# A hand-written schedule: weight preparation placed behind the second block's transposed queries

## The reference

```python
x = x + layernorm(attn(layernorm(x)))      # attn: h = h + global(rmsnorm(h)); h = h + local(rmsnorm(h))
x = x + layernorm(ffn(layernorm(x)))
# global: 16 query heads, 4 key heads of 8, latent keys and values, causal mask, rope and norm of q and k
# local:  the same head shape, each token sees the 32 tokens up to itself
# ffn:    h = layernorm(x) * gamma + beta
#         shared expert silu(h @ q(sw1).T) @ q(sw2).T, plus top_prob * expert[argmax router](h), 8 experts
#         q(W): scale = mean|W| per row;  clip(round(W / scale), -1, 1) * scale
```

## Time and profile before

| | |
|---|---|
| median of 3 runs | 808.54 us (807.95 to 810.76) |
| span of the profiled execution | 806.6 us |
| median less span | 1.9 us |
| PE matmul busy | 579.3 us, 72% of the span |
| DVE busy | 468.5 us, 58% |
| ACT busy | 363.7 us, 45% |
| POOL busy | 348.6 us, 43% |

### The profile page before, as it was taken

The page is one execution under the profiler, slowest core; times in us unless marked ns, Lnnn a source line. Parts: engine busy times, 40 slices in busy tenths (PEclk is TensorE's granted clock), DMA queues, the critical chain, the costliest instruction groups (busy, mean ns, idle before and its releaser), DMA issues.

```text
span 806.6 us, 15564 instructions
## 1 busy us (share of the span) xinstructions
PE 579.3 (72%) x5544; PEld 282.4 (35%) x5621; DVE 468.5 (58%) x1130; ACT 363.7 (45%) x482; POOL 348.6 (43%) x752
## 2 busy tenths in 40 slices
PE   1217727838688877989898898978898898665353
PEld 1103313416243434444434343433343332422241
DVE  5473867665678566676566745683266221656256
ACT  0013404423446436746675567647764787103000
POOL 3504786486335573557326432653004530045200
PEclk9956867978899989999999999999999999765566
DMA  7000000000000000000000000000000000000000
GB/s 207 1 0 1 1 2 1 1 1 2 1 8 1 2 1 8 2 2 5 4 2 1 5 5 2 2 4 5 2 2 1 8 2 1 1 0 8 1 0 7
DMA packets 8809, 6.20 MB, mean 8 GB/s; under 512 B 1816, under 2 KB 8096, under 8 KB 8736
## 3 DMA queue, kind: packets, MB, share of 16 engines
q10 hardware_dynamic: 3424, 2.69, 1.2%
q1 hardware_dynamic: 5312, 2.52, 1.2%
HBM read 4.16 MB, written 1.05 MB: 6 GB/s over the span
## 4 chain that ended last, share of the span: by engine, by line
PE 26%; POOL 25%; DVE 23%; issue 18%; another core or an unknown queue 5%; ACT 1%; DVEq 0%; SPq 0%; DMA 0%; POOLq 0%; ACTq 0%
PE osum_g L893 8%; POOL prob L677 8%; PE scores L869 7%; DVE qT L1213 3%; PE misc L990 3%; DVE early L1321 3%; PE misc L1001 2%; POOL qe_g L652 2%; DVE acc L1363 2%; POOL prob L670 1%; POOL qe_l L652 1%; POOL ke_g L657 1%; DVE early L1360 1%; POOL rs_g L600 1%
## 5 line engine op out<-in xcount | busy, mean ns | idle before, releaser
L739 ACT ACTIVATE prob<-scores 128x1024 f32<-128x1024 f32 (+3 forms) x352 | 314.8, 925 | 191.0 <-PE scores L869 146.1
L869 PE MATMUL scores<-qT,kT 128*128 128x512 bf16 (+3 forms) x693 | 179.1, 353 | 43.9 <-DVEq L1217 19.6
L893 PE MATMUL osum_g<-prob,V 128*32 128x256 f32 (+1 forms) x2304 | 171.9, 385 | 10.1 <-ACT prob L739 4.6
L677 POOL TENSOR_TENSOR prob<-prob,band 128x768 f32<-128x768 f32 (+1 forms) x64 | 98.8, 1574 | 80.1 <-ACT prob L739 80.1
L869 PEld LDWEIGHTS scores<-qT,kT 128*128 128x128 bf16 x760 | 50.9, 100 | 146.9 <-issue 118.0
L893 PEld LDWEIGHTS osum_g<-prob,V 128*32 128x32 f32 x2304 | 51.1, 109 | 97.4 <-issue 81.0
L670 POOL TENSOR_SCALAR_AFFINE_SELECT prob<-prob 128x512 f32<-128x512 f32 x64 | 41.2, 664 | 88.1 <-ACT prob L739 87.9
L1001 PE MATMUL misc<-t2T,h1p 128*128 128x512 bf16 x182 | 53.2, 451 | 24.8 <-DVE h1p L1353 19.9
L1213 DVE COPY qT<-misc 64x1024 bf16<-64x1024 bf16 x64 | 44.1, 689 | 13.6 <-PE misc L855 8.2
L990 PE MATMUL misc<-early,t1T 128*128 128x256 bf16 x384 | 47.5, 285 | 2.8 <-DVEq L1325 2.6
L893 PE MATMUL misc<-prob,V 128*32 128x128 f32 (+2 forms) x736 | 31.5, 288 | 18.5 <-POOL prob L677 18.0
(11 more groups left out here) (212 smaller groups left out, 838.5 us busy)
## 6 DMA issues: line engine op xcount, KB each, us to landing
X<-in_L_attn_hidden_dram SPq DMA_DIRECT2D x8, 128.0 KB, 5.0
early<-in_L_ffn_expert_w_dram ACTq DMA_DIRECT2D x1, 1024.0 KB, 7.3
out_dram<-X SPq DMA_DIRECT2D x16, 64.0 KB, 1.5
rope<-in_rope_dram SPq DMA_DIRECT2D x1, 256.0 KB, 3.5
early<-in_L_ffn_shared_w_dram ACTq DMA_DIRECT2D x2, 128.0 KB, 9.2
band<-in_band_dram ACTq DMA_DIRECT2D x1, 96.0 KB, 3.0
wraw_l<-in_L_attn_l_wq_dram ACTq DMA_DIRECT2D x1, 64.0 KB, 2.5
ident<-in_ident_dram SPq DMA_DIRECT2D x1, 64.0 KB, 2.3
```

The source lines that it names most:

```text
L677: pool.tensor_tensor(d, d, m.unsqueeze(1).broadcast_to([P, 4, n]), ALU.mult).then_inc(mask_done, 1)
L739: act.activation(prob[:, n % NP, :, lo:hi], src, ACT.Exp, scale=float(HD) ** -0.5).then_inc(exp_done, 1)
L869: ins = pe.matmul(o[:, :, c:c + w], kT[a][:, g, P * (t % kept[a]):P * (t % kept[a]) + P], qT[a][:, b % Q_KEPT[a], 2 * g + m, :, q:q + w], ...
L893: ins = pe.matmul(o[32 * m:32 * m + 32, q:q + w], V[a][:, t % kept[a], g, :], prob[:, n % NP, m, c:c + w], start=(first and k == 0), stop= ...
```

## The change

Two steps of the feed chain, `prep` and `ternary` 0, are not allowed until the second half of block 1's query transposition (`qT`, G, 1, 1) is in the list. The rule that the first local block needs `prep` moves from its projection to its norm. `prep` has a name of one element, for which `allowed` did not ask `reads_done`; now it does. No operation is added, removed or altered; only the list can differ.

```diff
     def reads_done(s):
 
+        if s in (("prep",), ("ternary", 0)):
+            return ("qT", G, 1, 1) in plan
         kind, a, *at = s
...
-        if kind == "proj" and a == L and ("prep",) not in plan:
+        if kind == "norm" and a == L and ("prep",) not in plan:
             return False
...
     def allowed(s):
-        return (s[0] != "qk" or room(2)) and (s[0] != "pv" or s[1:] in ended) and banks(s) and (len(s) == 1 or reads_done(s))
+        return (s[0] != "qk" or room(2)) and (s[0] != "pv" or s[1:] in ended) and banks(s) and (len(s) == 1 and s != ("prep",) or reads_done(s))
```

## The result

The changed kernel takes 828.72 us, median of 4 runs (824.93 to 830.83), against 808.93 us of the kernel before on the same chips: ratio 1.0258, 95% interval 1.0218 to 1.0298. It was forecast 8 us faster and is 20 us slower, outside the range. The profile after is of the fastest of the four (824.93 us), so the two traces differ by 16.6 us of span and not by 20.

A forecast was written before the change was run, and what follows sets the result against it. Bound by the PE stream from 200 to 700 us, by DVE and POOL block preparation from 78.8 to 112.7. Span 806.6 - 11.8 + 0 + 3.4 + 0 + 0 = 798.2, with 1.9 around it 800.1 us; range 789 to 811.

The forecast's parts named there:

- Step 1: Start of the kernel: preparation leaves the path of block 0's key copy, first scores at 44.7 us; -11.8 us.
- Step 2: Block 0's attention and block 1's copies: all moves forward in one piece; 0 taken, bounds 0 to -7 us.
- rival C: Better than a shift: block 1's copies move by 19 us instead of 12; 793.1 us, chance 0.14.
- Step 3: Preparation put back behind block 1's query copies, DVE idle time taking up part; +3.4 us, bounds 0 to +11.8.
- Step 4: First ternary step's eight compares at the new place, with POOL at work: no longer; 0 taken, other end 9.9 us.
- Step 5: Feed-forward weights slide by at least 26 us, first local block by at most 11.8; both covered, cost 0.
- Step 6: From 200 us to the end: the early gain is let through in full.
- The reservation: In step 6: the greedy planner makes all later choices anew, and in-order waits may vanish or appear; no size given.
- The sign named for this step: Step 6 is wrong if PE is 8 us ahead at 200 but not at 700, with PE under 86% between.
- Rival D: Slower: PE's in-order queue stops at a weight transpose early on; +8.0 us, 816.5 us, chance 0.13.

The follow-up runs named there:

- e1: Kernel before with its own list, only prep and ternary 0 moved behind block 1's second query transposition, nothing planned anew: 808.59 us, ratio 1.0006.
- e8: Kernel before's list with prep, ternary 0, the first weight transpose and ternary 1 moved behind global block 2's split: 810.88 us, ratio 1.0017.
- e11: As e10, with ternary 1, 2 and 3 also moved into DVE's wait ahead of block 2's norm: 795.43 us, ratio 0.9877.
- e10: Kernel before's list with prep right behind block 0's projection and ternary 0 right behind block 1's: 799.67 us, ratio 0.9906.
- e9: Kernel before's list, weight reductions replaced by constants and first ternary step by a memset, so not computing the reference: 799.78 us, ratio 0.9921.
- e2: Changed kernel's list with only prep and ternary 0 put back ahead of block 0's key transposition: 838.62 us, ratio 1.0360.
- e16: Changed kernel's list, local block, norms and feed-forward of blocks 0 to 2 and weight steps put back to old places by global-unit count: 892.26 us, ratio 1.1041.

## Why the prediction was wrong

- **Step 1** held: key copy at 40.83, first scores at 45.13, 11.4 us earlier.
- **Step 2** held, near its better bound: the statistics of block 2 got in ahead of the later masks, DVE's wait was 9.50 and not 14.82 us, and block 1's copies started 17 us earlier, 5 more than the shift. That reading belonged to rival C, which was right up to block 2's copies (24 us earlier) and wrong by 36 us at the end (793.1 forecast).
- **Step 3** was mis-sized for the old list: there the putting back costs 11.8 us and not 3.4 (e1, e8). In the changed list it can't be read apart, since block 2's copies came out more ahead than block 1's. DVE's 8.4 us of idle time between 78.8 and 112.7 were waits inside chains and took nothing up, and POOL binds the same stretch (e11). By these runs, idle time of a stretch is room only where something ready stands ahead of the wait in the queue. In e10 it did.
- **Step 4** held for what it looked at, the eight compares: 1.65 us at the new place, 0.21 us each. It overlooked the eight operations right behind them (L1089, which is L1087 in the kernel before). They started at 84.37 together with two of POOL's mask selects and took 2.99 us instead of 2.19. That is 0.8 us, small beside the rest.
- **Step 5** held for the weights: their scales were copied 27 us later (167.7 instead of 141.0), near the 26 that were estimated as the least. Nothing waited for them alone that a run could show. It was wrong for the first local block, which was to slide by at most 11.8 us: its output product stood at 184.4 instead of 149.9, and the first feed-forward transpose at 198.2 instead of 164.9, because the new list puts more global attention ahead of them.
- **Step 6** is the step that failed. "I let it through in full" is nearly true for a fixed list: in their traces e9 and e10 carry 8 to 9 us through 750 us of unchanged order, and their medians are 6 us under that of the kernel before on the same chip. It is false for a list planned anew. The reservation stood in the text and had no price in the sum or in the range; it measured +29 us (e2, 24 to 34 by its interval), more than all other terms together. Of the planner's clock I used only what it meant for the first hundred steps. The sign named for this step came true in its first half: up to 200 us the changed kernel has done 977 loads against 899, 78 ahead and so about 8 us, and up to 700 us 5207 against 5295. The second half did not: PE is busy 436.98 of 500 us from 200 to 700, 87% and not less than 86%. At a clock of 0.94 instead of 0.97 matmuls are longer, so the busy share stays up while less work is done. The busy share was the wrong sign to watch. That the move inside the new list comes out at the forecast 8 us (the changed kernel against e2) is agreement in number only: steps 3 and 5 were off on the way.
- **Rival D** had the right sign, less than half of the size (816.5) and the wrong reason: the changed kernel's longest wait of PE for ternary weights is 0.9 us. The wait does exist in e1, where the list is old.

What stays open is which feature of the changed order costs. It is shown that the loss against the kernel before builds up between 180 and 520 us, with more short waits of PE for masks and exponentials and a lower clock; and that moving the first local and feed-forward blocks forward by hand does not mend it. The last 161 steps of the changed list, from 1084 on, are those of before, and from the last global output product to the end it takes 117.7 us against 119.2, so the tail has no part in it.

## What to carry to other kernels

Where a greedy planner makes the order, a change of a rule has two effects: the work moved, and a new list from there on. Take them apart by moving the steps in the old list by hand, and by moving them back in the new one; here they were 0 or -8 us, and +29 us. To compare progress, count work done and not busy time, which a lower clock keeps up. An idle start is best filled with work that fits into waits which are there already, ahead of the first dependent step; work moved to a busy stretch came back at full length here.

## What was not expected of the hardware

The order alone moved the time by much: the same 5621 weight loads took from 793.8 us of span (e11) to 884.2 us (e16). The mean clocks were 0.898 and 0.855, but a mean over the span says little: the runs of the kernel before alone lie between 0.874 and 0.910, and the two profiled ones of before and after have 0.881 and 0.875. It is the stretch from 260 to 520 us where the order shows, 0.97 against 0.92.

Two engines' operations met where the prediction had not looked: the operation of block 2's normalisation took 0.64 us at 55.50, beside four of POOL's mask selects that ran from 55.42, and 0.34 us at 72.21 before, with no mask beside it. The Trainium skill (SBUF — State Buffer, the two separate sides) has the two engines hold their shared ports for a whole instruction in turn. The row fits that, and no run here took the masks away. Masks are not the only case: in e10 the eight compares, which took 1.65 us elsewhere, took 2.15 us at 35.35, while POOL was at its term expansions and first Newton steps.
